# Quantised rows of the last matmul: cast by ScalarE and transposed by a DMA instead of by TensorE

## The reference

```python
def _L0_ffn_ref(x, weight, bias):
    ...
    x_mat = quantize_e4m3(x2d, SCALE).astype(jnp.float16)
    w_mat = quantize_e4m3(weight, SCALE).astype(jnp.float16)
    out2d = (x_mat @ w_mat.T).astype(jnp.float32) * (SCALE * SCALE)
    out2d = out2d + bias
    return out2d.reshape(B, N, -1)
x = x + _L0_xattn_ref(_layernorm(x, axis=-1), ctx_1024, ctx_1024, L0_xattn_W_diff, L0_xattn_b_diff, L0_xattn_ln_g, L0_xattn_ln_b, L0_xattn_W1, L0_xattn_b1, L0_xattn_W2, L0_xattn_b2)
x = x + _L0_ffn_ref(_layernorm(x, axis=-1), L0_ffn_weight, L0_ffn_bias)
```

## Time and profile before

| | |
|---|---|
| median of 3 runs | 270.52 us (270.42 to 270.64) |
| profiled execution, its own time | 270.51 us |
| span in its trace | 268.5 us |
| TensorE matmuls busy | 210.2 us, 78% |
| VectorE busy | 220.8 us, 82% |
| ScalarE busy | 203.4 us, 76% |
| GpSimd busy | 156.2 us, 58% |

### The profile page before, as it was taken

The page is one execution under the profiler, slowest core; times in us unless marked ns, Lnnn a source line. Parts: engine busy times, 40 slices in busy tenths (PEclk is TensorE's granted clock), DMA queues, the critical chain, the costliest instruction groups (busy, mean ns, idle before and its releaser), DMA issues.

```text
span 268.5 us, 5871 instructions
## 1 busy us (share of the span) xinstructions
PE 210.2 (78%) x1767; PEld 179.0 (67%) x1767; DVE 220.8 (82%) x860; ACT 203.4 (76%) x731; POOL 156.2 (58%) x203
## 2 busy tenths in 40 slices
PE   2557666653698888885799999999999999999230
PEld 1456654433586666664699998999999898998120
DVE  1888999989969999999525788889988888879961
ACT  4499999998579999997856666677778666676520
POOL 2375777776666555573353577666666677755550
PEclk9999799995579999999999999999999999999755
DMA  5875555520000000000094347577888777774677
GB/s 152 231 146 163 164 153 168 154 76 1 1 0 2 2 0 5 2 0 2 0 103 57 35 47 78 75 97 104 122 118 119 105 100 105 94 95 73 119 109 148
DMA packets 44767, 22.33 MB, mean 83 GB/s; under 512 B 2240, under 2 KB 44608, under 8 KB 44736
## 3 DMA queue, kind: packets, MB, share of 16 engines
q0 software_dynamic: 16896, 8.39, 27.5%
q1 hardware_dynamic: 27408, 13.38, 19.3%
q10 hardware_dynamic: 432, 0.20, 0.3%
HBM read 9.37 MB, written 4.19 MB: 51 GB/s over the span
## 4 chain that ended last, share of the span: by engine, by line
PE 46%; DVE 23%; ACT 19%; DMA 4%; issue 4%; POOL 2%; SPq 0%; DVEq 0%; POOLq 0%; ACTq 0%
PE bank L884 21%; ACT TQK L415 6%; ACT TQK L431 6%; DVE q_c L663 6%; DVE F L686 6%; DVE LN_c L671 6%; PE bank L874 5%; PE bank L875 5%; PE bank L876 5%; DMA LN_c<-in_ctx_dram 3%; ACT PV L426 3%; PE bank L904 2%; ACT vT_c L420 2%; DMA F<-rows 2%; PE bank L829 1%
## 5 line engine op out<-in xcount | busy, mean ns | idle before, releaser
L884 PE MATMUL bank<-W2T,TQK 128*128 128x128 f32 x512 | 68.1, 279 | 0.0
L884 PEld LDWEIGHTS bank<-W2T,TQK 128*128 128x128 f32 x512 | 64.5, 191 | 4.1
L507 ACT ACTIVATE TQK<-bank,b1c 128x512 f32<-128x512 f32 x64 | 43.9, 687 | 24.4 <-PE bank L876 24.3
L336 POOL TENSOR_SCALAR q_c<-TQK,GAINK,SHIFT 128x128 f32<-128x128 f32 x64 | 32.1, 518 | 20.5 <-PE bank L849 19.9
L874 PE MATMUL bank<-hTh,W1h 128*128 128x512 f32 x64 | 29.2, 456 | 1.6 <-DVE hTl L759 1.6
L318 POOL TENSOR_TENSOR xrstd<-xvar,pow_c 128x4 f32<-128x4 f32 x16 | 16.8, 1052 | 23.0 <-DVE xvar L591 23.0
L377 POOL TENSOR_TENSOR ovar<-sso,eps_c 128x4 f32<-128x4 f32 x16 | 3.1, 192 | 44.5 <-ACT TQK L521 44.5
L875 PE MATMUL bank<-hTl,W1h 128*128 128x512 f32 x64 | 25.4, 396 | 0.0
L876 PE MATMUL bank<-hTh,W1l 128*128 128x512 f32 x64 | 25.2, 394 | 0.0
L783 PE MATMUL bank<-ident,LN_c 128*128 128x128 f32 x64 | 11.7, 312 | 17.1 <-DMA LN_c<-in_ctx_dram 17.1
L705 DVE TENSOR_TENSOR F<-bank,F 128x512 f32<-128x512 f32 x16 | 11.1, 691 | 16.9 <-PE bank L884 13.3
(11 more groups left out here) (119 smaller groups left out, 624.3 us busy)
## 6 DMA issues: line engine op xcount, KB each, us to landing
F<-rows POOLq DMA_DIRECT2D x32, 256.0 KB, 5.1
LN_c<-in_ctx_dram SPq DMA_DIRECT2D x16, 256.0 KB, 3.0
X<-in_x_dram SPq DMA_DIRECT2D x16, 256.0 KB, 3.4
out_dram<-F SPq DMA_DIRECT2D x16, 256.0 KB, 4.3
LN_c<-in_L_xattn_W_dram SPq DMA_DIRECT2D x1, 256.0 KB, 6.5
lT_c<-in_L_xattn_W_dram SPq DMA_DIRECT2D x1, 256.0 KB, 5.4
E_c<-in_L_xattn_W_diff_dram ACTq DMA_DIRECT2D x1, 64.0 KB, 3.1
rows<-in_L_xattn_b_diff_dram ACTq DMA_DIRECT2D x1, 64.0 KB, 5.5
```

The lines of the kernel that those rows point to most:

```text
L336: last = pool.tensor_scalar(tile(diff_c, k, i), all_tile(TK, k, i), per_tile(GAINK, k, i, 1), per_tile(SHIFT, k, i, 1), ALU.mult, ALU.add)
L507: act.activation(buf(hid_c, m, HB * C)[:, j * C:(j + 1) * C], M1_B[j % 2][:, :], ACT.Gelu, bias=b1c[:, j:j + 1]).then_inc(gelu_ready, 1)
L884: last = pe.matmul(M2_B[m.buf][:, i * D:(i + 1) * D], buf(hid_c, m, HB * C)[:, j * C + i * D:j * C + (i + 1) * D], W2T[:, j * D:(j + 1) * ...
```

## The change

ScalarE casts the fp8 rows to bf16, SBUF to SBUF, one step earlier (lag 4), into a new buffer `xq16_c`, which takes a part of LN_c that the third stage did not use. SP issues a DMA that transposes the four 128 x 128 tiles of `xq16_c` into `xqT_c`, and TensorE waits for that DMA at lag 5, just before the weight matmuls. The transposing matmuls and the copy of bank 5 are gone. The transposes stand in SP's queue among the stores.

```diff
+        xq16_c = LN_c[:, 3 * C:4 * C].bitcast(BF16)
...
-            def store(k):
-                wait(sp, y_ready, k.n + 1)
-                sp.dma_start(out_d[k.n], tiles(chunk(F, k))).then_inc(stored, 16)
-
-            for n in range(NC):
-                store(Chunk(n // 2, n % 2, 0, NC))
+            def phase3(at):
+                k = at(4)
+                if k.live:
+                    sp.wait_ge(xq16_ready, k.n + 1)
+                    wait(sp, ff_ps, k.n - 1)
+                    sp.dma_start_transpose(tiles(buf(xqT_c, k)), buf(xq16_c, k)).then_inc(xqT_in[k.buf], 16)
+                k = at(6)
+                if k.live:
+                    sp.wait_ge(y_ready, k.n + 1)
+                    sp.dma_start(out_d[k.n], tiles(chunk(F, k))).then_inc(stored, 16)
+
+            run_steps(sp, NC, 6, phase3)
...
-                h, m, o, q = at(0), at(1), at(2), at(5)
+                h, m, o, c, q = at(0), at(1), at(2), at(4), at(5)
...
+                if c.live:
+                    act.wait_ge(xq_ready, c.n + 1)
+                    if c.n > 1:
+                        act.wait_ge(xqT_in[c.buf], 16 * c.pair)
+                    act.activation(buf(xq16_c, c), buf(xq_c, c), ACT.Copy).then_inc(xq16_ready, 1)
                 if q.live:
-                    act.wait_ge(xqT_ps, q.n + 1)
-                    wait(act, ff_ps, q.n - 1)
-                    act.activation(buf(xqT_c, q), XQ_B[:, :], ACT.Copy).then_inc(xqT_sb, 1)
                     act.wait_ge(ff_ps, q.n + 1)
...
-                    wait(dve, xqT_ps, q.n - 1)
+                    wait(dve, xq16_ready, q.n - 1)
...
-                if q.live:
-                    pe.wait_ge(xq_ready, q.n + 1)
-                    wait(pe, xqT_sb, q.n)
...
-                if q.live:
-                    for i in range(G):
-                        last = pe.matmul(XQ_B[:, i * D:(i + 1) * D], tile(xq_c, q, i), ident8[:, :],
-                                         start=True, stop=True)
-                    last.then_inc(xqT_ps, 1)
...
-                    pe.wait_ge(xqT_sb, q.n + 1)
+                    pe.wait_ge(xqT_in[q.buf], 16 * (q.pair + 1))
```

More of the change, by code:

```diff
@@ L251, in xattn_ffn_kernel @@
             sem("x1_rstd"))
-        xq_ready, xqT_ps, xqT_sb, ff_ps, r16_ready, y_ready = (
-            sem("xq_ready"), sem("xqT_ps"), sem("xqT_sb"), sem("ff_ps"), sem("r16_ready"), sem("y_ready"))
+        xq_ready, xq16_ready, ff_ps, r16_ready, y_ready = (
+            sem("xq_ready"), sem("xq16_ready"), sem("ff_ps"), sem("r16_ready"), sem("y_ready"))
+        xqT_in = [sem(f"xqT_in{i}") for i in range(2)]
         stored = sem("stored")
```

## The result

The changed kernel took **267.93 us** (median of 7 runs, 266.64 to 269.68) against 270.52 us before (7 runs, 269.79 to 270.64): 2.59 us less, ratio 0.990 with a 95% interval of 0.9874 to 0.9926. Repeated on another chip the ratio was 0.9936 (0.991 to 0.9963), on a third, from two runs, 0.9896 (0.9862 to 0.993). So it is faster, by 0.6 to 1.0% in the three, with intervals from 0.4 to 1.4%. I had forecast 269.4, 1.1 us less; the gain came out more than twice that. Its profiled execution took 267.95 us, 2.56 less than that of before.

What follows compares the result with a forecast made beforehand. The prediction took TensorE to bound the third stage's full steps, with the end set by chunk 15's bias DMA. It summed 270.51 - 2.42 (matmuls removed) + 1.27 (transpose at the end) = 269.36, so 269.4 us, range 267.9 to 276.0.

Steps and rivals of the forecast that it cites:

- (1): Full steps of the third stage: TensorE loses the transposing matmuls L908, 0.22 us in each of 11 steps, 2.42 us less.
- (2): ScalarE behind gelu(3): the cast replaces the copy L530 of 0.59 us; even 0.69 would vanish in 0.98 idle.
- (3): Full steps, cast to weight matmuls: one transposing DMA per chunk goes unfelt up to 7.63 us from issue to landing.
- (4): SP's queue: stores wait behind the cast and the transpose's issue, but only the end waits for a store: 0.
- (5): DMA engines in full steps: a transpose adds 0.5 to 2.3 us to 5.85; costs 0 in the steady steps.
- (6): The end, chunk 15: the transpose path costs T - 3.03 us against the last bias DMA, nothing below T = 3.03.
- T: Time of a transposing DMA from issue to landing, taken as the stores' 4.3 us, with bounds 2.9 and 8.8.
- Rival A: The end: the transpose is free there, T at most 3.03, total 268.1 us; chance 0.05.
- B: The tail: the four blocks go one behind another, T 7.4 us, total 272.5; taken as T 4.9 to 7.63, chance 0.30.
- C: Full steps: TensorE waits in every step, T over 7.63; at T = 8.8 the total is 286.7 us; chance 0.16.
- D: Full steps: the 0.22 us gain doesn't come because ScalarE's chain binds instead, total 271.8 us; chance 0.07.

Runs made afterwards that it cites:

- the doubled version: The changed kernel with every transpose done twice, the second issued after the first landed, TensorE waiting for the second: 274.52 us, ratio 1.0143.

## Why the prediction was right or wrong

- **What bounds, and where the gain lies**: right. TensorE bounds the full steps before and after, eleven of them hold the gain, and steps, cast and queue behaved as said.
- **(1), 11 x 0.22 = 2.42 us: the first mis-sized term.** The step lost 0.28, and eleven of them 3.09. Removing L908 also shortened what stands behind it, `mlp2`'s first group, from 0.95 to 0.89 in the chain. That 0.95 stood in the trace of before; its like elsewhere in the same step took 0.89. I priced the removed row alone and not what its neighbours cost because of it: 0.67 us missed.
- **(2), the cast at no cost**: right; 0.62 us, inside 0.95 of idle time.
- **(3), the cover of 7.63 us**: nothing speaks against it. 4.3 us did not show, and 7.3 cost 0.6 us over eleven steps.
- **(4), SP's queue**: right for the change. It does cost where SP has to wait for a landing in the last steps, which the doubled version showed.
- **(5), the DMA engines**: the load was 0.8 us a step, between the bounds, and nothing in the full steps waited. What the DMAs do to each other at the end was left out of the sum, and there it has a price of up to 1.2 us.
- **(6) and T, priced at 1.27 us: the second mis-sized term, with the wrong mechanism in part.** 4.3 us was the median of the transposes to the tenth, but only in the full steps. The one T in the sum is the last, and it was 2.9 to 3.7 us. I had taken it from the stores' median over the whole stage, not from the end's own traffic. For the full steps the reason given holds, that both run beside the same accumulates: without the bias DMAs the stores fall to 2.9 and T to 2.4. With T - 3.03 the end would have cost at most 0.7; what it did cost, 0.3 to 1.1, came in two of three executions from the bias DMA. It takes 4.39, 4.43 and 4.47 us in three traces without a transpose beside it (before, L908 moved, transposes taken out), and 4.67, 5.50 and 5.0 in the changed kernel. I had put that stretching at nothing.
- **The sum**: -3.09 + 0.3 (to 1.1) = -2.8 (to -2.0), against -2.42 + 1.27 = -1.15. Both terms erred the same way, by 0.67 and 0.98. In this pair of traces the start took 0.41 back, and 0.17 came from behind the last addition and outside the span: 2.39 + 0.17 = 2.56 us, as measured. Rival A, which I had given 0.05, is the case that came in this execution, with T = 2.94 and the last addition released by the bias DMA; in the other two T was 3.7. That its 268.1 is so near to the measured 267.9 is luck: it lacks the 0.67 of the steps, the 0.29 of the end and the 0.41 of the start, which nearly cancel. Rivals B, C and D had 0.53 between them; none came.
- **What the pages gave**: the Trainium skill's "VectorE: DVE Perf Modes", section "The three transpose paths", gives 1309 ns for one block, so four in a row would be an estimated 5.2 us (its advice for TensorE stands in the section "Rules for kernel authors"). This case's trace has 2.4 us for all four, without the bias DMA beside it and with the issue in it. By the Trainium skill's "Advanced Engine Details and Errata", section "X-Bar Transpose (TRN2)", transposing DMAs are as fast as regular ones. The trace without the bias DMAs agrees for what comes behind the issue: 2.4 - 1.2 = 1.2 us for 128 KB, where the stores of 256 KB took 2.9 - 0.58 = 2.3. The issue itself is twice as long, 1.2 against 0.58 us.

## What to carry to other kernels

A transpose that TensorE does in a step it bounds can go to the DMA queue if a whole step lies between its data and its use: here 4.3 us under a cover of 7.6. At the ends of the pipeline the same DMA has no cover and stretches the DMA beside it, so here the last chunks were better left to TensorE. Price a DMA by the traffic around that one issue, not by the median of its stage; and when an instruction is taken out, look at what its neighbours cost more than their like.

## What the runs showed of the hardware

- A transposing DMA of 128 x 512 bf16 in SBUF takes 2.42 us from issue to landing without the bias DMA beside it, 1.2 us of it on SP's sequencer, which issues the store of twice the bytes there in 0.58. In the full steps of the changed kernel the issue alone took 1.5 us.
- Beside an accumulating DMA of 256 KB it takes 4.3 us in the full steps, and the accumulate at the end goes from 4.39 to as much as 5.59. There each is slowed by the other; in the full steps the accumulate isn't (5.2 before, 4.8 after), and the store behind the transpose is (4.4 and 5.4).
- The fp32 matmuls right after fp8 or bf16 ones cost 0.05 to 0.06 us more in the chain than their like (0.95 against 0.89 for a group of eight, 0.28 against 0.23 for one of 512 columns); two short groups side by side pay that once (step 7.45 against 7.50).
